# A Mamba block with ternary FFNs: the FFN bias moves from GpSimd to a TensorE product, and one more state's addition from VectorE to ScalarE and GpSimd

## The reference

```python
x = x + 0.5 * ffn(layernorm(x))        # ternary weights, scale = mean|W|, plus bias
x = x + mamba(layernorm(x))            # in-projection, conv of 4 taps, scan with 16 states, gate, out-projection
x = x + 0.5 * ffn(layernorm(x))        # the same ternary weights and bias
```

## Time and profile before

| | |
|---|---|
| median of 3 runs | 3069.3 us (3067.49 to 3071.17) |
| profiled execution, its time | 3067.46 us |
| profiled execution, its span | 3065.6 us |
| mean granted TensorE clock over the span | 0.908 |
| second pass | from about 1122 us to the end |
| busy in the second pass, 1300 to 3000 us | DVE 98%, POOL 91%, PE 85%, ACT 66% |

### The profile page before, as it was taken

One profiled execution on the slowest core, in us unless ns is written; L12 is line 12 of the kernel. 1 busy time (PEld: TensorE's weight loads), 2 busy tenths in 40 slices (PEclk: granted clock), 3 DMA queues, 4 the chain that ended last, 5 costly groups with the idle time before them and its releaser, 6 DMA issues.

```text
span 3065.6 us, 42581 instructions
## 1 busy us (share of the span) xinstructions
PE 2471.9 (81%) x12448; PEld 1411.2 (46%) x12448; DVE 2586.4 (84%) x3383; ACT 1887.5 (62%) x3366; POOL 1954.7 (64%) x1577
## 2 busy tenths in 40 slices
PE   3568889889898636888888888888888888888887
PEld 1233344444343224555455555555555555555453
DVE  6566767767766559999999999999999999999993
ACT  2333756756756766666666666666666666666663
POOL 1111222222221148898999999989989989989983
PEclk8689999999999857798999998999999999999999
DMA  6552323332332262221221221221222222212101
GB/s 209 185 211 104 129 99 106 120 106 105 111 109 93 81 238 78 76 73 59 87 77 47 86 87 46 79 82 62 76 74 70 76 67 80 73 59 90 59 28 42
DMA packets 159747, 286.75 MB, mean 94 GB/s; under 512 B 40897, under 2 KB 90305, under 8 KB 157185
## 3 DMA queue, kind: packets, MB, share of 16 engines
q1 hardware_dynamic: 159488, 283.71, 27.6%
HBM read 174.09 MB, written 109.58 MB: 93 GB/s over the span
## 4 chain that ended last, share of the span: by engine, by line
POOL 34%; issue 15%; DVE 11%; PE 2%; POOLq 1%; ACT 1%; DMA 0%; SPq 0%; DVEq 0%; ACTq 0%
POOL dbu L1037 25%; DVE h L1246 7%; DVE y L1258 3%; POOL y L1054 3%; POOL o L1079 2%; POOL x L1073 2%; PE p_g L1371 1%; POOL carry L1048 1%; POOL y L1069 1%; POOL dbu L1042 1%; POOLq L40 1%; PE p_g L1361 0%; POOL small L69 0%; PE p_ht L1337 0%; DVE q L1271 0%
## 5 line engine op out<-in xcount | busy, mean ns | idle before, releaser
L1142 ACT ACTIVATE p_da<-dt_,neg_a 128x255 f32<-128x255 f32 x2048 | 885.6, 467 | 561.1 <-DVE h L1246 559.4
L1246 DVE TENSOR_TENSOR_SCAN h<-p_da,dbu 128x512 f32<-128x512 f32 x1024 | 1190.9, 1204 | 38.5 <-ACT p_da L1142 16.6
L1037 POOL TENSOR_TENSOR dbu<-dtu,bb 128x1024 f32<-128x1024 f32 x512 | 1197.3, 2360 | 0.6
L1337 PE MATMUL p_ht<-ident,h 128*128 128x128 f32 x4096 | 607.5, 307 | 212.0 <-DVE h L1246 209.8
L1337 PEld LDWEIGHTS p_ht<-ident,h 128*128 128x128 f32 x4096 | 535.8, 160 | 315.1 <-issue 164.0
L1258 DVE SCALAR_TENSOR_TENSOR y<-p_ht,ct,y 128x1024 f32<-128x1024 f32 x432 | 544.1, 1260 | 2.6 <-PE p_ht L1337 2.5
L1371 PE MATMUL p_g<-wo,tokt 128*128 128x512 f16 x1536 | 353.5, 388 | 1.6 <-ACT tokt L1174 1.6
L358 POOL TENSOR_TENSOR late<-dt,u 128x512 f32<-128x512 f32 x64 | 82.4, 1287 | 425.4 <-DVE dt L550 425.4
L1380 PE MATMUL p_g<-wz,xz 128*128 128x512 f16 x1536 | 350.6, 386 | 0.0
L706 PE MATMUL p_u<-xz,wu 128*128 128x512 f16 x1536 | 350.3, 386 | 0.0
L69 POOL TENSOR_TENSOR small<-small,consts 128x1 f32<-128x1 f32 x96 | 56.6, 589 | 433.3 <-DVE small L62 421.7
(11 more groups left out here) (119 smaller groups left out, 2997.5 us busy)
## 6 DMA issues: line engine op xcount, KB each, us to landing
bb<-b_scratch SPq DMA_DIRECT2D x128, 256.0 KB, 3.3
xin<-in_x SPq DMA_DIRECT2D x32, 512.0 KB, 4.3
x_scratch<-x SPq DMA_DIRECT2D x32, 512.0 KB, 3.3
xz_scratch<-xz SPq DMA_DIRECT2D x16, 1024.0 KB, 5.8
y_scratch<-late SPq DMA_DIRECT2D x32, 512.0 KB, 2.9
dt_scratch<-dt SPq DMA_DIRECT2D x64, 256.0 KB, 2.2
dtu_scratch<-late SPq DMA_DIRECT2D x64, 256.0 KB, 2.5
dt_<-dt_scratch SPq DMA_DIRECT2D x64, 256.0 KB, 3.5
```

The lines of the kernel that those rows point to most:

```text
L1037: nc.gpsimd.tensor_tensor(state[:, 4 * f:4 * f + 4, :], dtu[par][:, 4 * f:4 * f + 4, :], bb[n // NB % 2][:, n % NB:n % NB + 1, :].to_broad ...
L1142: ins_ = nc.scalar.activation(p_da[p % 2][:, k * T2 + 1:(k + 1) * T2], dt[:, g, 1:], ACT.Exp, scale=neg_a[:, g, n:n + 1])
L1246: nc.vector.tensor_tensor_scan(h[n % 2][:, 2 * p:2 * p + 2, :].rearrange("p g t -> p (g t)"), p_da[p % 2][:], dbu[n % 2][:, 2 * p:2 * p + ...
L1337: mm = nc.tensor.transpose(p_ht[t][:, g * P:(g + 1) * P], h[n % 2][:, g, t * P:(t + 1) * P], ident[:])
```

## The change

The bias is no longer added by POOL. In each "f" unit PE first puts `ident` (128x128, f32) times 512 columns of the bias into the bank, and the 16 f16 products accumulate on it. Since the bank is scaled by `ffn_scale` on its way out, the bias is divided by that scale before; the scale is worked out in the DVE prologue of the first pass, with two small instructions more, and is kept above a tiny value. `finish` waits for `xn_done` instead of the bias's semaphore. The parted states of tile 1 are now 3, 5, 7, 9, 11 and 13, and POOL adds them in slots 8, 10, 12, 14 and in slots 0 of the next turn.

```diff
-                    nc.vector.tensor_scalar(consts["ffn_scale"], tmp[:, 3, 0:1], 0.5 / XS, None, ALU.mult)
+                    link(nc.vector.tensor_scalar(consts["ffn_scale"], tmp[:, 3, 0:1], TINY_SCALE, 0.5 / XS, ALU.max, ALU.mult))
+                    link(nc.vector.reciprocal(tmp[:, 3, 3:4], consts["ffn_scale"]))
+                    nc.vector.tensor_scalar(consts["bias_scale"], tmp[:, 3, 3:4], 0.5, None, ALU.mult)
...
-        PARTED = (3, 5, 8, 10, 13)
-        PART_ADDED = {8: 5, 11: 8, 13: 10}
+        PARTED = (3, 5, 7, 9, 11, 13)
+        PART_ADDED = {8: 5, 10: 7, 12: 9, 14: 11}
...
-                def add_bias(c, t):
-                    wait(pool, xn_done, c * TT2 + t + 1)
-                    nc.gpsimd.tensor_tensor(x1[t][:], x1[t][:], half_bias[:], ALU.add).then_inc(xb_done, 1)
-
                 def finish(i, c, t, x):
                     b, m = place(i, "f", t, x)
                     wait(pool, g_free[b], m + 1)
-                    wait(pool, xb_done, c * TT2 + t + 1)
+                    wait(pool, xn_done, c * TT2 + t + 1)
...
-                            if n == 5:
-                                add_bias(i - 2, 1)
...
-                            if n == 12:
-                                if isinstance(i, int) and i == 1:
-                                    pool.wait_ge(bias_done, 1)
-                                add_bias(i - 1, 0)
...
-                                nc.scalar.mul(half_bias[:], half_bias[:], 0.5).then_inc(bias_done, 1)
+                                nc.scalar.activation(half_bias[:], half_bias[:], ACT.Copy, scale=consts["bias_scale"]).then_inc(bias_done, 1)
...
                     if kind == "f":
                         for a in range(2):
                             wait_evac(i - t, "n", t, a)
+                        if isinstance(i, int) and i == 1:
+                            pe.wait_ge(bias_done, 1)
+                        nc.tensor.matmul(p_g[b][:], ident[:], half_bias[:, cols], start=True, stop=False)
                         for g in range(G):
                             for a in range(2):
                                 mm = nc.tensor.matmul(p_g[b][:], tokt[:, a, g, :], tern[:, g, cols],
-                                                      start=(n == 0), stop=(n == 2 * G - 1))
+                                                      start=False, stop=(n == 2 * G - 1))
```

More of the change, by code:

```diff
@@ L30 @@
 TINY = 1e-30
+TINY_SCALE = 1e-20
 EPS = 1e-5
@@ L842, in second_pass @@
             sem(n) for n in ("ln2_chain", "stats2_ready", "pow2_done", "scale2_ready", "xn2_done"))
-        xb_done, fin_done = sem("xb2_done"), sem("fin_done")
+        fin_done = sem("fin_done")
         o_stored = [sem(f"o_stored{i}") for i in range(2)]
@@ L1432, in macaron_block @@
         c = ctx.enter_context(nc.sbuf_tensor("consts", [P, 8], F32))
-        consts = {n: c[:, k:k + 1] for k, n in enumerate(("ffn_scale", "u_scale", "half_z", "out_scale", "minus_half"))}
+        consts = {n: c[:, k:k + 1] for k, n in enumerate(("ffn_scale", "u_scale", "half_z", "out_scale", "minus_half", "bias_scale"))}
         with nc.sbuf_tensor("wu", [P, 2, G, D], F16) as wu_t:
```

## The result

The changed kernel takes 3074.01 us in the median of 16 runs (3071.36 to 3077.61), the kernel before on the same chips 3068.55 us (3066.77 to 3071.58, 16 runs). The ratio is 1.0017, with a 95% interval of 1.0010 to 1.0024: 5.2 us more (3.1 to 7.4). The centre is just inside what I called no change (6.1 us), and the sign is sure. The forecast was +3.4 us and 3072.7 us. The profiled execution took 3072.83 us, its span is 3071.0 us (before 3065.6).

A forecast was written before the change was run, and what follows sets the result against it. The prediction took DVE, 98% busy in the second pass, as the bound, with POOL close behind. Its terms, +0.4 - 1.2 - 2.1 + 1.2 + 5.1 = +3.4 us, gave 3072.7 us, called same; overall range 3065 to 3082.

The forecast's parts named there:

- Slots 8 to 13, -2.1 us: Second pass, 15 chunks: skips save 1.18 us each, but DVE waits 1.04 for state 11's decays; 0.14 gained a chunk.
- The bare skip in slot 12: Slot 12, nothing of DVE between its last scan and state 13: decays in time by 0.1 us, no wait.
- PE late in slot 9, +1.2: DVE asks for state 8's turned columns 1.18 us earlier and waits 0.4 us for PE in three chunks.
- The chunk of turn 0, -1.2: Second-pass chunk with no layer norm beside it: it keeps its gain of 1.2 us.
- POOL, 0 with a margin of 1.0 left at state 15: Removed bias additions gain nothing; the slot 14 addition halves the margin of state 15's dbu to 1.0 us, no wait.
- The product in the loop, 0: PE's f32 bias product in the second pass's f units is covered by PE's idle time, costing 0.
- The end, +5.1: Three uncovered pairs of f units on the last path, each longer by two products of 0.86 us: +5.1 us.
- The start, +0.4: Two more linked 128x1 instructions ahead of the ternary weights, 0.20 us each: +0.4 us.
- the gain is kept: Rival, chance 0.12: state 11's decays come early enough, all 16 x 1.18 us count: -13.4 us, 3055.9 us.
- Product costs double: Rival, chance 0.10: the six products at the end run at the lower clock, +5.1 us more, 3077.8 us.
- POOL late: Rival, chance 0.07: additions in slots 10, 12, 14 delay POOL past its margin at state 15; 3082 us taken.
- ACT not covered: Rival, chance 0.07: ACT's state 9 work delays the second rounding by 1.0 us, DVE waits 2.0 us; 3088 us.

The follow-up runs named there:

- experiment 2: Changed kernel with the bias added by POOL again, the six parted states kept: 3070.38 us, ratio 1.0004 to the kernel before.
- experiment 3: Changed kernel with parted states 3, 5, 8, 10, 11, 13, so DVE keeps state 9's addition and skips state 11's: 3054.53 us, 0.9952 to the kernel before.
- experiment 9: Changed kernel without parting state 9 (parted 3, 5, 7, 11, 13; 432 DVE additions): 3076.46 us, ratio 1.0025 to the kernel before.
- experiment 1: Changed kernel with the bias product on PE kept but the old parted states 3, 5, 8, 10, 13: 3074.51 us, ratio 1.0015 to the kernel before.
- experiment 7: Changed kernel with PE's f32 bias product done twice in each of the 64 FFN units: 3082.67 us, ratio 1.0049 to the kernel before.
- experiment 10: Changed kernel with seven parted states (3, 5, 7, 8, 10, 11, 12) and the bias product ahead of PE's waits: 3031.58 us, 0.9879 to the kernel before.
- experiment 6: Changed kernel with parted states 3, 5, 8, 10, 11, 13 and the bias product ahead of PE's waits: 3053.06 us, 0.9952 to the kernel before.

## Why the prediction held, and where it didn't

It held in its main claim, and experiments 2, 3 and 9 show the reason: state 11 gives the saved addition back. Term by term:

- **Slots 8 to 13, -2.1 us: mis-sized, it was +3.7** (all six slots, by the starts of the scans). The place and the releaser were right in all 15 chunks. The step that failed is the chain's length, taken as a constant from one chunk in which all of PE's links ran at full clock. The kernel before had that length in only seven of 15 chunks, so the margin of 0.14 us was no margin in the other eight; in the change the links are 0.2 us longer in seven chunks and 0.7 in eight. "The second rounding stays at 2255.9 or slips by 0.1; I take 0" was right: ACT's work on state 9 is covered. The bare skip in slot 12 costs nothing, as taken.
- **PE late in slot 9, +1.2: wrong.** DVE's waits for turned columns grew by 0.3 us in all, in the whole second pass. I set DVE's coming earlier and left PE's start where it was, but PE turns what DVE has scanned, so the two come forward together. This is a reading of the order; no run tested it.
- **The chunk of turn 0, -1.2: wrong.** It kept 0.1: DVE waits 0.56 us for POOL's dbu, and 1.18 and 0.54 for ACT, where before it waited 1.31 in all.
- **POOL, 0 with a margin of 1.0 left at state 15: right.** Its dbu is done at 2287.77, DVE comes at 2288.68, 0.9 later. The removed bias additions bring nothing (experiment 1).
- **The product in the loop, 0: right.** None of the 64 products (two records each) has a waiter in the profile.
- **The end, +5.1: the mechanism right, the net +2.8.** Three times 1.7 us is there row for row, and experiment 7 gives it again by doubling. I took the rest of the end as fixed; the clock of the first out-projection was not.
- **The start, +0.4: right.** The linked steps read 20.53, 20.73, 20.92, 21.11. The first pass as a whole is 1.3 us shorter beside that, with no single place for it.

In the sum the misses are +5.8 at slots 8 to 13, +1.1 in turn 0, -0.9 in slot 9, -2.3 at the end and -1.3 in the first pass; and +1.4 at the turns of the loop, -2.2 in slot 3 and +0.4 in other slots, of which I had nothing. They make +2.0, from the forecast +3.4 to the +5.4 of the spans. So the sum is nearer than its terms, and that is luck.

The rival "the gain is kept", with the rule of the Trainium skill beside it (Perfetto Trace Analysis, "Optimizing Scalar/DVE Operations": with a saturated DVE, moving work to Scalar may make sense), is refuted for this change (experiment 2, 1.0004) and borne out with other slots (experiment 3, 0.9952; experiment 10, 0.9879). The rule tells which engine to relieve, not at which instruction. "Product costs double" is out by 3004.02 and experiment 7 for these kernels; in experiment 3 the last pair's first product did run slow once, in 1.86 us. "POOL late" is out by its margin, and "ACT not covered" by the chunk of experiment 2.

What stays open is what decides TensorE's clock at such places, in the chain and at the end. Both kernels without the product have a slow first out-projection at the end (12.80 before, 12.91 in experiment 2), eight of the ten with it have none, and experiment 6 (13.41) and experiment 9 (12.21, in the second) do. So the product may help the clock there, or it may be chance; each kernel has one profile, and no run here tells it apart.

## What to carry to other kernels

On a saturated engine, one instruction less is worth its step only if the next one's inputs are ready that much sooner; ask for each candidate slot what chain ends there, and whether it begins on the same engine a little earlier, in which case the instruction is cover and not load. Here the change with its six offloaded additions gave +5.2 us, and -14.7 us with two of the six at other states. Read a chain's length in every chunk and not in one or three, and take it as a range, since a link's duration can change with the clock, and look in the unrolled start and end for costs that the loop hides.

## What was unexpected of the hardware

- PE's short links between two DVE instructions run at either level of the clock, chunk by chunk in one and the same loop: the four transposes take 0.66 or 1.12 us, with a granted clock of 1.00 (2255 to 2257 before) or 0.55 (2256 to 2258 after) around them. In the kernel before at least one link was slow in 8 of 15 chunks, in the change in all 15; a chunk of the change with all of them slow costs DVE about 0.45 us more than one in which the transposes are quick.
- The same 48 matmuls at the end took 10.52, 12.80 or 13.41 us in different kernels; in their first 4.5 us the clock was 1.00 in the change and 0.50 in the kernel before. That is 2.3 to 2.9 us in a single place, where the whole change costs 5.2.
- An f32 product of 128x512 costs PE 0.86 us at full clock, the same whether alone or doubled. It is the time of four f16 products of its size (3.45 us for 16).
